# Cross-attention and mixture-of-experts block on one core: record scatters issued one by one between GpSimd's other calls, output bias as a TensorE row product, context loaded already transposed, and a new order of calls on every engine

## What is computed

```python
# x, ctx: (32, 128, 256); 16 heads of width 16; 8 experts, hidden width 1024
q, k, v  = heads(layernorm(x) @ Wq + bq), heads(ctx @ Wk + bk), heads(ctx @ Wv + bv)
scores   = alpha * 4 * (q . k) / (|q| + |k|) ** 2          # per head, per pair of tokens
x        = x + (softmax(scores) @ v).merge() @ Wo + bo
y        = layernorm(x)
w, idx   = top_k(softmax(y @ Wr), 2);  w = w / sum(w)
out      = x + sum over the 2 experts of w * (gelu(y @ W1[e] + b1[e]) @ W2[e] + b2[e])
```

## Time and profile before

| | us |
|---|---|
| median of the runs shown (1051.5 to 1056.38, three runs) | 1053.28 |
| the profiled execution, its own time | 1048.44 |
| its span | 1046.7 |
| TensorE busy in the span | 929.1 (89%) |
| DVE busy | 688.0 (66%) |
| ACT busy | 637.1 (61%) |
| GpSimd busy | 433.3 (41%) |

### The profile page before, as it was taken

One profiled execution on the slowest core, in us unless ns is written; L12 is line 12 of the kernel. 1 busy time (PEld: TensorE's weight loads), 2 busy tenths in 40 slices (PEclk: granted clock), 3 DMA queues, 4 the chain that ended last, 5 costly groups with the idle time before them and its releaser, 6 DMA issues. The chain is left out here.

```text
span 1046.7 us, 30647 instructions
## 1 busy us (share of the span) xinstructions
PE 929.1 (89%) x10734; PEld 814.2 (78%) x10734; DVE 688.0 (66%) x1806; ACT 637.1 (61%) x1234; POOL 433.3 (41%) x572
## 2 busy tenths in 40 slices
PE   2699999998989979989988707999999999999994
PEld 1588887886877868868867506999999999999994
DVE  5357787785866857957758543566666666666663
ACT  0478888885966867858758403555555555555551
POOL 4235466556455564563544620233222222222222
PEclk9799999998998989989989757999999999999997
DMA  4202223122222332341332227433333333233322
GB/s 126 80 29 67 82 68 113 45 83 93 84 64 77 114 96 95 107 149 33 113 128 99 97 84 302 135 58 58 49 53 49 52 49 53 49 51 52 52 34 26
DMA packets 61893, 84.96 MB, mean 81 GB/s; under 512 B 9744, under 2 KB 55312, under 8 KB 59568
## 3 DMA queue, kind: packets, MB, share of 16 engines
q1 hardware_dynamic: 46976, 63.33, 18.9%
q0 software_dynamic: 13296, 18.00, 10.3%
q10 hardware_dynamic: 1472, 1.67, 0.6%
HBM read 49.99 MB, written 31.92 MB: 78 GB/s over the span
## 5 line engine op out<-in xcount | busy, mean ns | idle before, releaser
L1442 POOL DMA_INDIRECT out<-yw,rb x71 | 111.0, 1564 | 308.8 <-DVE yw L1413 228.5
L1375 ACT ACTIVATE h<-s_ps,b1t,inv 128x128 f32<-128x128 f32 x288 | 106.8, 458 | 89.8 <-PE s_ps L1326 88.9
L1375 ACT ACTIVATE h<-u_ps,b1t,inv 128x128 f32<-128x128 f32 x280 | 103.5, 461 | 87.4 <-PE u_ps L1326 86.6
L1396 DVE TENSOR_SCALAR hs<-h,hsc 128x512 f16<-128x512 f32 x142 | 69.3, 488 | 119.8 <-ACT h L1375 116.2
L647 ACT ACTIVATE pt<-gen,escale 128x512 f32<-128x512 f32 x128 | 85.7, 681 | 42.8 <-PE gen L433 21.3
L1398 DVE SCALAR_TENSOR_TENSOR hs<-h,hsc,hs 128x512 f16<-128x512 f32 x142 | 106.7, 751 | 5.1
L1326 PE MATMUL s_ps<-xt,w1s 128*128 128x128 f16 x1728 | 105.6, 221 | 2.6 <-issue 1.8
L1326 PEld LDWEIGHTS s_ps<-xt,w1s 128*128 x1728 | 100.7, 99 | 3.5 <-issue 3.0
L901 DVE SCALAR_TENSOR_TENSOR tw<-th,s_ps 128x1024 f32<-128x1024 f32 x64 | 77.9, 1218 | 38.2 <-PE s_ps L416 20.3
L1340 PE MATMUL pv_ps<-w2s_sb,hs 128*128 x864 | 100.6, 273 | 0.8 <-issue 0.7
L1326 PE MATMUL u_ps<-xt,w1s 128*128 128x128 f16 x1680 | 99.6, 219 | 0.0
(11 more groups left out here) (234 smaller groups left out, 1817.7 us busy)
## 6 DMA issues: line engine op xcount, KB each, us to landing
wl<-L_ffn_W SPq DMA_DIRECT2D x16, 1024.0 KB, 5.6
rb<-xrec SPq DMA_DIRECT2D x71, 132.5 KB
w2s<-wst SPq DMA_DIRECT2D x8, 1024.0 KB, 9.1
w2s_sb<-w2s SPq DMA_DIRECT2D x8, 1024.0 KB, 15.0
xin<-x SPq DMA_DIRECT2D x32, 128.0 KB, 3.6
cin<-ctx SPq DMA_DIRECT2D x32, 128.0 KB, 2.1
xres<-x SPq DMA_DIRECT2D x32, 128.0 KB, 4.0
out<-x SPq DMA_DIRECT2D x32, 128.0 KB, 2.0
```

The costliest lines, as they stand in the source:

```text
L1375: ins = act.activation(h32[n % HBANKS][:, m % HB, :], hbank[n % HBANKS][:, o:o + SLOT], ACT.Gelu, scale=inv1[:, bass.ds(ex, 1)].bitcast(F3 ...
L1396: dve.tensor_scalar(hi, h, scale, None, ALU.mult).then_inc(sig("hi"), 1)
L1442: pool.indirect_dma_start(out[:, :], bass.IndirectOffsetOnAxis(ap=rb[j][:, D + NE:D + NE + 1], axis=0), yw[s % 2][:, :], None, compute_op= ...
```

## The change

- **Scatters.** `scatter(p)`, which issued eight indirect DMAs in a row, becomes `scatter(t, i, p)`, which issues one. Two of the eight (group 0) stand at the end of GpSimd's iteration p + 2, the other six in iteration p + 3 between `norm_again`, `record_low` and the `split_max` calls.
- **Output bias.** `add_bias` and `xb` go. `project_out` begins with a row product: a 96-row matrix of ones times `bop`, which holds bo + bv @ Wo in three bfloat16 parts. `residual` on DVE adds `xres` directly. Set-up work on DVE splits `bo_sb` into `bop`.
- **Context.** The host stores ctx with tokens in columns, a change of layout alone. SP loads it to where the product reads it, `cin` now holds two pairs and is read by `project` directly; TensorE's transposes of `cin` go, and ACT's copy `xct` is 256 wide, not 512.
- **Order.** All five loops and `TURNS` are written in a new order. On DVE the counts per expert become a call of their own, `counts`, right behind `choose`; `shares` and `positions` of the scatters' pair now open the even iterations and `choose`, `counts` the odd ones, ahead of `scores(0)`; `weight_low` also stands ahead of `scores(0)`.

```diff
-            def scatter(p):
+            def scatter(t, i, p):
                 m = p // 2
+                pool.wait_ge(*at("rtok", m + 1))
                 pool.wait_ge(*at("ridx", m + 1))
                 for b in range(2):
                     pool.wait_ge(*at(f"rl{b}", p + 1))
-                for t in range(4):
-                    for i in range(2):
-                        pool.indirect_dma_start(xrec_d[:, :], bass.IndirectOffsetOnAxis(ap=idx[:, i, t:t + 1], axis=0),
-                                                rec[m % 2][:, t, :], None).then_inc(sig("scat"), 16)
+                pool.indirect_dma_start(xrec_d[:, :], bass.IndirectOffsetOnAxis(ap=idx[:, i, t:t + 1], axis=0),
+                                        rec[m % 2][:, t, :], None).then_inc(sig("scat"), 16)
```

```diff
             def project_out(b, p):
                 g = pe_turn(pe, f"wo{b}", p)
+                if p == 0 and b == 0:
+                    pe.wait_ge(*at("set_bo", 2 * NSPLIT + 1))
+                pe.matmul(g[:, 0:D], ones_b[0:RROWS, :], bop[:, :], start=True, stop=False)
                 pe.wait_ge(*at("ote", 2 * p + b + 1))
                 for k in range(DC):
-                    ins = pe.matmul(g[:, 0:D], ot[:, k, :], wo_sb[:, k, :], start=(k == 0), stop=(k == DC - 1))
+                    ins = pe.matmul(g[:, 0:D], ot[:, k, :], wo_sb[:, k, :], start=False, stop=(k == DC - 1))
...
             def norm(b, p):
                 g = pe_turn(pe, f"xct{b}", p)
                 pe.wait_ge(*at(f"xn{b}", p + 1))
-                pe.wait_ge(*dma(f"ldc{b}", p + 1))
-                for i, src in enumerate((xn[b], cin[b])):
-                    for k in range(DC):
-                        o = (DC * i + k) * P
-                        ins = pe.transpose(g[:, o:o + P], src[:, k * P:(k + 1) * P], idf[:, :])
+                for k in range(DC):
+                    ins = pe.transpose(g[:, k * P:(k + 1) * P], xn[b][:, k * P:(k + 1) * P], idf[:, :])
...
+            for i in range(NSPLIT):
+                row = slice(i * STRIP, i * STRIP + 1)
+                dve.wait_ge(*at("set_bo", 2 * i + 1))
+                dve.tensor_copy(bot[:, :], bo_sb[0:RROWS, :]).then_inc(sig("set_bo"), 1)
+                dve.wait_ge(*at("set_bo", 2 * i + 2))
+                ins = dve.tensor_copy(bop[row, :], bot[row, :])
+                if i + 1 < NSPLIT:
+                    ins = dve.tensor_tensor(bo_sb[0:RROWS, :], bo_sb[0:RROWS, :], bot[:, :], ALU.subtract)
+                ins.then_inc(sig("set_bo"), 1)
...
-            def add_bias(b, p):
-                pool.wait_ge(*dma(f"ldr{b}", p + 1))
-                if p:
-                    pool.wait_ge(*at(f"x1{b}", p))
-                pool.tensor_tensor(xb[b][:, :], xres[b][:, :], bo_sb[:, :], ALU.add).then_inc(sig(f"xb{b}"), 1)
```

More of the change, by code:

```diff
@@ new lines, in tensor_program @@
+                if 0 <= it < NP:
+                    factors(2, it)
+                if 0 <= it - 1 < NP:
+                    project_out(1, it - 1)
+                if 0 <= it < NP:
+                    scores(2, it)
+                    factors(3, it)
+                if 0 <= it + 1 < NP:
+                    project(0, it + 1)
+                if 0 <= it < NP:
+                    turned(1, 0, it)
+                    weight_products(it)
+                if 0 <= it - 1 < NP:
+                    logits(0, it - 1)
@@ new lines, in tensor_program @@
+                if 0 <= it < NP:
+                    scores(3, it)
+                    values(0, it)
+                    weight_sum(it)
+                    turned(1, 1, it)
+                if 0 <= it - 1 < NP:
+                    turn_y(1, it - 1)
+                if 0 <= it < NP:
+                    turned(2, 0, it)
+                if 0 <= it + 1 < NP:
+                    rows(it + 1)
+                if 0 <= it < NP:
+                    values(1, it)
+                if 0 <= it + 2 < NP:
+                    norm(0, it + 2)
@@ L959, in choose, with counts @@
                 dve.tensor_tensor(rs["d"][:, :], rs["l2"][:, :], rs["l1"][:, :], ALU.subtract).then_inc(sig("rd"), 1)
+            def counts(p):
+                m = p // 2
+                if m:
+                    dve.wait_ge(*at("rank", m))
+                step(dve.tensor_tensor(hot[:, :, :], f("oh1"), f("oh2"), ALU.add))
+                step(dve.tensor_copy(acc2[:, 0, :], acc_cnt[:, :]))
+                for t in range(1, 4):
+                    step(dve.tensor_tensor(acc2[:, t, :], acc2[:, t - 1, :], hot[:, t - 1, :], ALU.add))
+                dve.tensor_tensor(acc_cnt[:, :], acc2[:, 3, :], hot[:, 3, :], ALU.add).then_inc(sig("racc"), 1)
             def shares(p):
@@ L1023, in weight_exponent @@
                 dve.tensor_scalar(wsc[:, :], wkk[:, :], -float(ONE), 268.0 * ONE, ALU.mult, ALU.add).then_inc(sig("wsc"), 1)
-            for it in range(-3, NP + 2):
+            for it in range(-2, NP + 3):
                 if 0 <= it - 1 < NP:
                     heads_back(0, it - 1)
-                    weight_exponent(it - 1)
+                if 0 <= it - 3 < NP and it % 2 == 0:
+                    shares(it - 3)
+                    positions(it - 3)
+                if 0 <= it - 2 < NP and it % 2:
+                    choose(it - 2)
+                if 0 <= it + 2 < NP:
+                    means(0, it + 2)
+                if 0 <= it - 1 < NP:
+                    weight_low(it - 1)
+                if 0 <= it - 2 < NP and it % 2:
+                    counts(it - 2)
                 if 0 <= it < NP:
@@ L1217, in gpsimd_program @@
                     record_low(0, it - 2)
+                if 0 <= it < NP:
+                    split_max(0, it)
                 if 0 <= it - 1 < NP:
                     norm_again(0, it - 1)
+                if 0 <= it - 3 < NP and it % 2 == 0:
+                    scatter(1, 0, it - 3)
                 if 0 <= it + 2 < NP:
                     norm(1, it + 2)
+                if 0 <= it - 2 < NP:
+                    record_low(1, it - 2)
+                if 0 <= it - 3 < NP and it % 2 == 0:
+                    scatter(1, 1, it - 3)
+                if 0 <= it < NP:
+                    split_max(1, it)
+                if 0 <= it - 1 < NP:
+                    norm_again(1, it - 1)
+                if 0 <= it - 3 < NP and it % 2 == 0:
+                    scatter(2, 0, it - 3)
+                if 0 <= it < NP:
+                    split_max(2, it)
+                if 0 <= it - 3 < NP and it % 2 == 0:
+                    scatter(2, 1, it - 3)
+                    scatter(3, 0, it - 3)
+                    scatter(3, 1, it - 3)
+                if 0 <= it + 1 < NP:
+                    units(it + 1)
+                if 0 <= it < NP:
+                    split_max(3, it)
+                if 0 <= it - 2 < NP and it % 2:
+                    scatter(0, 0, it - 2)
+                    scatter(0, 1, it - 2)
             pool.wait_ge(*dma("scat", 4 * NP))
```

306 lines of the change are left out of this document (123 added, 183 removed), and 16 rows, old and new, of the table TURNS.

## The result

The changed kernel takes 1013.97 us (median; 1012.29 to 1016.11), the kernel before in the same comparison 1053.99. The ratio is 0.962, with a 95% interval of 0.959 to 0.9653: 40 us faster. The profiled execution took 1016.11 us, with a span of 1014.3. It is the slowest of the four, while the profiled one before, at 1048.44, was faster than all four runs of the comparison.

What follows compares the result with a forecast made beforehand. TensorE, busy 89% of the span, was taken to bound the kernel, with stalls and clock dips at the scatter blocks. 1048.4 - 36 + 3 - 3 + 2 - 4 = 1010.4, plus 4.8 for the median: 1015 us, range 998 to 1040.

Steps and rivals of the forecast that it cites:

- 36 us for the stalls: First stage, 15 periods: 507.2 us against 470.8 if all were clean; spreading the scatters gains 36 us if no stall is left.
- The scatters' cost: GpSimd in the first stage: spread scatters cost 3 us through split_max(0) coming late, bounds 0 and 28.
- The clean length: First-stage iterations without scatters: 31.83 or 32.00 us, bounded by TensorE; ten periods were counted at 32.0.
- The TensorE term: TensorE in the first stage: 0.26 us less per iteration from context and bias, 3 us taken, bounds 0 and 4.
- The new order: Order of calls in all loops: TensorE's idle 1.2 us per clean iteration could go or double, -18 to +18; 0 taken.
- Held scatters: Rival, chance 0.17: scatters and split_max held beside DVE's instructions, TensorE waits up to 1.9 us per iteration, 1025 to 1045 us.
- The late signal: Rival, chance 0.10: indirect DMAs close together still delay ACT, seven pairs lose 7.4 us each, 1055 to 1080 us.
- the scatters don't spread: Rival, chance 0.05: GpSimd runs behind, so its scatters follow each other as before; about 1050 us.
- everything is better than clean: Rival, chance 0.10: the new order also takes TensorE's idle 1.2 us per iteration, 1000 +- 3 us.
- Context and bias: First stage: two transposes of cin per block go, row products are added; with GpSimd freed of add_bias, 3 us gained.
- Set-up, 2 us: DVE's three splitting rounds ahead of the first statistics: 2 us lost, bounds 1 to 4.
- End of stage one, 4 us gained: GpSimd takes the last-but-one block's statistics 3.9 us late behind scatters; the new order gains 4 us, bounds 0 and 5.

Runs made afterwards that it cites:

- b_spread: Kernel before with only GpSimd's loop changed: the eight scatters go one or two at a time over both iterations of a pair; 1001.87 us, 0.9519.
- a_bunched: Changed kernel with all eight scatters in a row again, at the head of GpSimd's even iterations; 1068.5 us, 1.0147.
- a_single: Changed kernel with only GpSimd's loop changed: all eight scatters in the even iteration, no two next to each other; 997.65 us, 0.95.
- b_spread_ctx_bias: Kernel before with scatters spread one or two at a time, context in columns and bias on TensorE, old order of the other calls; 1001.35 us, 0.9512.
- a_group0_later: Changed kernel with scatters (0, 0) and (0, 1) moved into the even iteration, behind split_max(0) and norm_again(0); 1014.72 us, 0.9638.
- b_ctx_bias: Kernel before with context in columns and output bias on TensorE, old order and block of eight scatters kept; 1056.95 us, 1.0036.
- b_plain: Kernel before with scatters spread in the old order, plus an ordinary GpSimd DMA behind (0, 0) and (0, 1); 1004.06 us, 0.956.
- b_run3: Kernel before with scatters spread in the old order, but (0, 0), (0, 1), (1, 0) in a row ahead of split_max(0); 1006.85 us, 0.9572.

## Why the prediction came out right

**The mechanism.** The prediction said that the loss of the kernel before sat in GpSimd's block of eight, as a late signal and a held maximum, followed by a clock dip, and that spreading removes it. b_spread and a_bunched show this from both sides: the block costs 51 us in the old order, and its return costs some 54 us in the new one (1068.5 against 1013.97).

**The total.** 1015 against 1013.97 is closer than the sum deserves. For the profiled execution it gave 1010.4, 38.0 less than before, and that execution took 1016.11, 32.3 less. The 4.8 us added on top, by which the profiled execution of the kernel before lies under its median, would have had to be -2.1 for the kernel after. These two misses cancel, and so do two larger ones inside the sum.

**The sum, 36 us for the stalls.** The term was measured from weight copy to weight copy, 507.2 against 470.8 if every iteration were clean. After, the same stretch takes 472.6. But it hides the two larger misses:

- The scatters' cost was put at 3 us with bounds of 0 and 28. The six even periods exceed 30.5 us by 3.8, 3.7, 3.7, 3.7, 5.2 and 0.7, 21 in all. 0.6 us of each is TensorE's own routing work, so some 17 are the stalls; the fifteen periods of a_single are 17.5 shorter (463.38 against 480.90).
- The clean length was put at 32.0. At 30.47 in mid-stage, with 30.2 for the first and 25.5 for the last period, the clean sum is 451.8, 19 us below my 470.8. The TensorE term, 3 us taken, explains 4: 30.30 against 30.02 busy, 0.28 times 15. The rest is idle time and the reference itself. Of the three windows that I called clean, two were touched by the first block of scatters, which starts at 169: 32.00, the value that I took for ten periods, is one of them. b_spread, with the old order, has a mean period of 31.2 in mid-stage, so 0.8 us per iteration was hidden in my reference. The scatters explain it only in part: the window of 31.83, which holds none, is also above 31.2, and why was not tried. Fifteen times 0.8 are 12 of the 22 us by which b_spread came out better than I expected; another 6 are my taking 30 of the 36.

**The new order, 0 with bounds of -18 and +18.** The runs split it. With single scatters the new order may be a little better than the old one: by the medians 3.7 us (a_single 997.65, b_spread_ctx_bias 1001.35), but the intervals of the two ratios overlap. In the profiles it is 6.9 us of span, of which 2.2 lie in the periods; that of a_single is its fastest run and the other one the slowest of its four, and b_spread_ctx_bias has two of its scatters in a row. As it was written, with a run of three and with (0, 0) beside the weight product, it is worse than the same kernel in the old order by 12.4 us of span. So the order was no small matter, and the loss lies in two places for scatters, not in the order of TensorE, ACT or DVE.

**The rivals.** Held scatters were real: the scatter beside the weight product takes 3.19 us, and TensorE waits 8.3 us in all for the maximum. The prediction named the holder, `weight_low`, and the size of one hold, 1.9 us against 2.2. The late signal was real as well: of the three in a row I had written that they might cause it from the first pair on, and they do, in all six even iterations of mid-stage. What was wrong was its price. I took a full 7.4 us for each; it is 1.6 us of TensorE's idle time at L425, since the signal of L506 comes 2.4 us late, where that of L433 came 4.4 us late before, TensorE has other work for part of it, and the clock holds through most of these short stalls. That the scatters don't spread, and that everything is better than clean, did not happen; a_single is the kernel that the last rival described (1000 +- 3), at 997.65.

On the first of them a rule was weighed. The trace shows a scatter held for 2.2 us by a DVE instruction with two inputs in SBUF, and a_group0_later shows the hold gone when the scatter is moved from beside it (mean 1054 ns against 1235). The Trainium skill, SBUF — State Buffer, section Who interferes with whom, says that one of the two engines gets the shared port pair for the whole instruction while the other is blocked; the trace agrees that the hold lasts to the end of DVE's instruction (the scatter ends 0.99 us behind it, which is the length of a free one). The same section infers that a `tensor_tensor` with both inputs in SBUF leaves the writing of descriptors alone; for this scalar_tensor_tensor with two inputs in SBUF the trace shows a DMA's issue held, so that inference doesn't carry over to it.

**Context and bias.** 3 us gained on TensorE and 2 lost in the set-up were forecast. With the scatters spread it is 1.7 gained in the periods, 2.5 lost in the set-up and 1.6 at the end. The measured ratio can't tell the pair from nothing. In b_ctx_bias it is slightly slower, 0.36%; in the profiles, where its own is the slowest of ten runs, the set-up is 2.1 us longer and the fifteen periods 7.5, with one late signal more; why a slightly shorter iteration meets the block worse was not tried.

**Set-up, 2 us.** The first statistics come 4.2 us later than before (24.45 against 20.23), outside my bounds of 1 to 4 by a little; in the experiments on the kernel after, with the same set-up, they come at 23.15 to 23.61. But the first tanh is only 0.5 us later, less than kernels with one set-up differ by. The cost at one step was not the cost at the step that counts.

**End of stage one, 4 us gained.** Wrong. From the last exponential to the first product of stage two it takes 51.20 us, against 49.99, so nothing was gained. That 1.2 us were lost is not shown: in the old order b_spread takes 49.08 and b_plain 50.80, and in the new one a_single takes 49.80. (From the first tanh of pair 15 it is 1.5 us less than before, in the calls ahead of the last exponential.) The 3.9 us that the block held at the end before concerned block 0 of the last pair; block 1's statistics came at 597.82 and were taken 0.24 us later, and it is block 1 that sets the end. There was nothing to gain. What TensorE waits for there is in the timeline of the kernel after, around block 1's `heads_back` (L928):

```profile
553.25 2.35 DVE L1025 SCALAR_TENSOR_TENSOR wst<-wl,wsc,wst 128x2048 f16<-128x2048 f32 x1
554.13 2.44 POOL L1199 DMA_INDIRECT xrec<-rec,idx  x1 [5.26 <-DVE idx L1010]
...
556.99 0.49 DVE L928 TENSOR_TENSOR on<-gen,rz 128x128 f32<-128x128 f32 x2
...
557.62 0.41 PE L460 MATMUL gen<-idf,on 128*128 128x128 f32 x2 [3.08 <-DVE on L928]
```

In the last turn no `scores(0)` needs the early place of the routing and of the weight product, but they keep it, ahead of block 1. TensorE waits 3.08 us for L928. a_single has the same wait of 3.1 us. That moving the product would win it back was not tried.

**The checks listed ahead.** A clock of 1.00 from 100 us to the end of stage one held but for one dip: the window of 35.68 us has 0.95, which is half clock for about 3.6 us (35.68 x 0.05 x 2). "No wait of L647 on a remote releaser" failed (11.3 us, four times), and the mean of a scatter, 1235 ns, was the sign named for held scatters. Iterations of 31 to 32 us throughout did not come; an iteration over 33 us at full clock was named as a sign that something is wrong, and it was one. The reason that I gave for such a case, DVE's routing or a load, was not it.

## What to carry to other kernels

A series of indirect DMAs on GpSimd should be spread one by one, with something else between any two and none of them right behind a long DVE instruction with two SBUF inputs. Here spreading by itself is worth 51 us of 1053 (b_spread), and in the new order the place of a few of them decides 13 to 16 us. Before a DMA is moved later, look at who waits for its landing, not only at what it waits for. And a "clean" iteration taken as the reference must be one from the time before the disturbance begins; a total that comes out right may hold two terms that are each over 15 us off.

## What the runs showed of the hardware

- TensorE's completion can reach ACT and DVE late while GpSimd issues indirect DMAs close behind each other. They wait up to 4.4 us with a remote releaser in a run of eight (before), 2.8 in a run of three (after), 1.7 in a run of three at another place (b_run3). With two in a row and an ordinary DMA or two additions behind them no such wait is listed, and the signal of L416 is still 1.1 to 1.2 us late. In a_bunched, also a run of eight, no signal of TensorE is over 0.7 us behind the modelled end. The one remote wait that b_spread has, 1.54 us of ACT at 543.75, fits: at the end of stage one, where the other calls of the loop fall away, four scatters follow each other from 537.86 to 542.8 just ahead of it.
- A scatter that starts beside DVE's product of 2048 float16 elements per partition takes 3.19 us (after), most others 0.96 to 1.11.
- A DMA that GpSimd issues takes 0.61 us of it if ordinary and 1.0 if indirect, for the same 128 rows of 265 words.
